# Edge scores of a graph layer: the first half's maximum ahead of the one-hots

## What is computed

```
src = jnp.concatenate([edge_index[0], loops])
dst = jnp.concatenate([edge_index[1], loops])
alpha = jax.nn.leaky_relu(s[src] + s[dst], NEG_SLOPE)
m = jax.ops.segment_max(alpha, dst, num_segments=N)
e = jnp.exp(alpha - m[dst])
denom = jax.ops.segment_sum(e, dst, num_segments=N)
a = e / denom[dst]
msg = Vh[src] * a[:, :, None]
attn = jax.ops.segment_sum(msg, dst, num_segments=N).reshape(N, D_MODEL)
```

## Time and profile before

| what | us |
|---|---|
| median of 3 runs | 2734.74 (2731.53 to 2736.45) |
| the profiled execution | 2739.28 |
| its span, first to last instruction | 2737.2 |
| PE busy | 1815.5 (66%) |
| DVE busy | 1752.0 (64%) |
| POOL busy | 1643.0 (60%) |
| ACT busy | 573.9 (21%) |
| scores of layer one (L690) | 108 to 251 |
| scores of layer two (L690) | 1450 to 1752 |
| messages of layer two (L1164) | 1885 to 2447 |

### The profile page before, as it was taken

One profiled execution on the slowest core, in us unless ns is written; L12 is line 12 of the kernel. 1 busy time (PEld: TensorE's weight loads), 2 busy tenths in 40 slices (PEclk: granted clock), 3 DMA queues, 4 the chain that ended last, 5 costly groups with the idle time before them and its releaser, 6 DMA issues. The chain is left out here.

```text
span 2737.2 us, 36321 instructions
## 1 busy us (share of the span) xinstructions
PE 1815.5 (66%) x10655; PEld 1474.6 (54%) x10655; DVE 1752.0 (64%) x2694; ACT 573.9 (21%) x1106; POOL 1643.0 (60%) x1456
## 2 busy tenths in 40 slices
PE   2795046777655554999886777405677777757688
PEld 1674034555444443699875555403555555546577
DVE  6689335777544447455675666796567777758675
ACT  2463100000000002354412222203000000004454
POOL 3477777887877773100007777788888888850050
PEclk8797567888877776799989999857788889878899
DMA  3266544554333333000023666733454444440010
GB/s 139 58 214 204 178 120 147 167 159 157 105 92 93 92 92 96 1 1 0 18 79 105 213 213 218 244 98 103 152 162 159 158 159 154 132 118 9 5 43 31
DMA packets 118702, 320.73 MB, mean 117 GB/s; under 512 B 37113, under 2 KB 63121, under 8 KB 104811
## 3 DMA queue, kind: packets, MB, share of 16 engines
q0 software_dynamic: 62272, 170.01, 21.9%
q1 hardware_dynamic: 55754, 145.31, 15.1%
q10 hardware_dynamic: 608, 4.59, 0.4%
HBM read 248.70 MB, written 71.12 MB: 117 GB/s over the span
## 5 line engine op out<-in xcount | busy, mean ns | idle before, releaser
L800 POOL DMA_INDIRECT e_ring<-table,e_index x840 | 1081.5, 1288 | 257.6 <-issue 256.1
L1187 PE MATMUL ms_ps_m<-ms_msg,ms_pick 128*128 128x260 f32 (+1 forms) x2816 | 859.7, 474 | 480.3 <-issue 266.5
L1187 PEld LDWEIGHTS ms_ps_m<-ms_msg,ms_pick 128*128 128x128 f32 x2816 | 659.0, 239 | 680.9 <-issue 532.8
L839 POOL DMA_INDIRECT e_ring<-table,e_stage_index x416 | 422.1, 1015 | 125.9 <-issue 120.9
L1164 DVE TENSOR_TENSOR ms_msg<-e_ring,all_xn 128x1040 f32 x176 | 217.8, 1237 | 354.0 <-SPq L1128 354.0
L690 PE MATMUL sc_ps_e<-sc_keys,sc_hot 125*128 125x100 bf16 (+1 forms) x3840 | 280.9, 229 | 86.8 <-DVE all_xn L643 86.5
L690 PEld LDWEIGHTS sc_ps_e<-sc_keys,sc_hot 125*128 125x128 bf16 x3840 | 254.7, 98 | 136.7 <-DVE all_xn L643 109.4
L1164 DVE TENSOR_TENSOR ms_msg<-e_ring,e_weight 128x1056 f32 x176 | 220.6, 1253 | 168.1 <-SPq L1128 168.0
L1160 DVE SCALAR_TENSOR_TENSOR ms_pick<-graph_dst_col,graph_tile_base,graph_lane_row 128x512 f32<-128x512 f32 x352 | 263.1, 748 | 11.4 <-issue 9.8
L605 ACT ACTIVATE sc_rows<-sc_ps_b 125x512 bf16<-125x512 f32 x320 | 173.0, 596 | 322.8 <-PE sc_ps_b L678 321.2
L643 DVE TENSOR_REDUCE all_xn<-sc_ps_e 128x800 f32 (+1 forms) x240 | 229.1, 982 | 1.4 <-PE sc_ps_e L690 1.3
(11 more groups left out here) (421 smaller groups left out, 2668.6 us busy)
## 6 DMA issues: line engine op xcount, KB each, us to landing
ahead<-e_ring SPq DMA_DIRECT2D x32, 1056.0 KB, 4.4
e_ring<-ahead SPq DMA_DIRECT2D x32, 1056.0 KB, 5.0
ahead<-e_ring SPq DMA_DIRECT2D x20, 1040.0 KB, 4.5
e_ring<-ahead SPq DMA_DIRECT2D x20, 1040.0 KB, 5.0
e_ring<-table,e_index POOLq DMA_INDIRECT x840, 2.8
e_ring<-table,e_stage_index POOLq DMA_INDIRECT x416
w_w<-L_ffn_w SPq DMA_DIRECT2D x2, 2048.0 KB
table<-qkv_v SPq DMA_DIRECT2D x5, 528.0 KB
```

Source lines behind the costliest of these rows:

```text
L800: pool.indirect_dma_start(out=g.ring[:, slot * QUAD + i // GT, i % GT, :], out_offset=None, in_=s.table[:, :], in_offset=bass.IndirectOffs ...
L839: pool.indirect_dma_start(out=stage.rows[:, b, t, :], out_offset=None, in_=s.table[:, :], in_offset=bass.IndirectOffsetOnAxis(ap=stage.ind ...
L1187: mm = pe.matmul(ps_m[b][:, 0:W], pick[:, b, t, :], msg[:, b, t, :], start=t == 0, stop=t == GT - 1)
```

## The change

VectorE's order in the scores. `select` now does one half; `turn_item` takes the maxima of all halves but the last, then makes the one-hots of the item after the next, then takes the last half's maximum. The first two items' one-hots are made before the loop, and the last four items stand after it. No wait is dropped or added: each instruction keeps its own condition. The other engines' instructions are the same and in the same order.

```diff
--- before.py
+++ after.py
@@ -636,11 +636,18 @@
                     dve.wait_ge(looked, (it - (HOTS - 1)) * SUBS)
                 dve.tensor_scalar(hot[0:KEYS, q % HOTS, :], rows[0:KEYS, q, :], s.node_of[0:KEYS, 0:1], None, ALU.is_equal).then_inc(hot_ready, 1)
 
-            def select(it, q):
-                for sub in range(SUBS):
-                    dve.wait_ge(looked, it * SUBS + (sub + 1))
-                    found = ps_e[(q * SUBS + sub) % BANKS][:, :].rearrange("p (t c) -> p t c", c=SLOT)[:, :, 0:C].rearrange("p t (g h) -> p t h g", h=H)
-                    dve.tensor_reduce(edge[:, bass.ds(it * ITEM + sub * SL, SL), :], found, AX.X, ALU.max).then_inc(picked, 1)
+            def select(it, q, sub):
+                dve.wait_ge(looked, it * SUBS + (sub + 1))
+                found = ps_e[(q * SUBS + sub) % BANKS][:, :].rearrange("p (t c) -> p t c", c=SLOT)[:, :, 0:C].rearrange("p t (g h) -> p t h g", h=H)
+                dve.tensor_reduce(edge[:, bass.ds(it * ITEM + sub * SL, SL), :], found, AX.X, ALU.max).then_inc(picked, 1)
+
+            def turn_item(it, q, more=True):
+
+                for sub in range(SUBS - 1):
+                    select(it, q, sub)
+                if more:
+                    one_hot(it + HOTS, (q + HOTS) % lanes, False)
+                select(it, q, SUBS - 1)
 
             dve.memset(pair[:, :, :, :], 0.0).then_inc(pair_zero, 1)
             dve.tensor_scalar(which[:, :], s.lane_row[:, :], LOW - 0.5, s.node_of[:, 0:1], ALU.is_ge, ALU.is_equal).then_inc(which_set, 1)
@@ -657,16 +664,13 @@
                 at = first // BANK_HI * TB
                 found = ps_e[0][0:LOW, at:at + (his.stop - his.start) * 3 * H].rearrange("p (g i h) -> p i g h", i=3, h=H)
                 dve.tensor_copy(keys[0:LOW, :, his, :], found).then_inc(keys_ready, 1)
+            for q in range(HOTS):
+                one_hot(q, q, True)
+            with steps_of(dve, 0, NITEM - lanes, lanes) as it0:
+                for q in range(lanes):
+                    turn_item(it0 + q, q)
             for q in range(lanes):
-                one_hot(q, q, True)
-                if q >= 2:
-                    select(q - 2, q - 2)
-            with steps_of(dve, lanes, NITEM, lanes) as it0:
-                for q in range(lanes):
-                    one_hot(it0 + q, q, False)
-                    select(it0 + (q - 2), (q - 2) % lanes)
-            for it in range(NITEM - 2, NITEM):
-                select(it, it % lanes)
+                turn_item(NITEM - lanes + q, q, q + HOTS < lanes)
 
         @block.tensor
         def _(pe):
```

## The result

The changed kernel takes **2740.23 us** (median of 7 runs, 2738.61 to 2746.47), the kernel before 2734.74 (7 runs, 2731.53 to 2736.45): a ratio of 1.0025, 95% interval [1.0014, 1.0037]. Forecast were 2737.9 in a range of 2730 to 2744 and "within 0.2%" as the likeliest outcome. The time lies in the upper part of the range. At a quarter of a per cent slow, the likeliest outcome, "within 0.2%", was narrowly missed on the slow side. The execution that was profiled took 2738.61 us, span 2736.5.

A forecast was written before the change was run, and what follows sets the result against it. The prediction took GpSimd's stream of 628 gathers to bound layer two; −1.6 + 4.8 = +3.2 us on the profiled 2739.28 gave 2742.5, or 2737.9 in terms of the median 2734.74, range 2730 to 2744.

The forecast's parts named there:

- The bound: Layer two ends when GpSimd has issued its 628 gathers, 975.2 us from first to last, which cover the shorter scores.
- Rival A: Message stage of layer two: VectorE's late start sets the end, so 76 us show, 2659 us; with partial gains chance 0.08.
- The period: Scores of layer two: 2.8 us an item against 3.78, so the scores shorten by 76 us and end near 1676.
- The first message product: Start of layer two's message stage: near 1857 us, not 1885, after VectorE stands some 45 us for rows.
- One-hots against gathers, +4.8: Scores of layer two: 80 more closely spaced one-hots lengthen gathers at layer one's price, +4.8 us, bounds 0 and +16.7.
- rival B: Parked gathers in layer two's scores: one-hots always start just ahead of a gather, +15 us, 2750 us; chance 0.15.
- The weights, 0 ± 2: Weights stage and accumulator clearing: VectorE's operations delay gathers as before, their price carried, 0, bounded by ±2 us.
- The first message groups, -1.6: Start of the message stage: without a stock of rows about 10 groups cost gathers 0.62 us each, not 0.78: −1.6 us.
- The sum: End of GpSimd's stream in layer two: −1.6 + 4.8 = +3.2 us, with what follows it unchanged.
- Rivals C and D: C: TensorE's clock falls in layer two's scores, up to 100 us slower, chance 0.02. D: same order, excluded for layer two.
- The page on the ports: GpSimd's gathers: by the skill page only one-hots disturb them, so −1.6 falls away, leaving +4.8 us, 2739.5.
- Wrong if a gather's mean is above 1040 ns: Gathers in layer two's scores: a mean near 1000 ns was expected; above 1040 ns would show one-hots meeting gathers in step.

The follow-up runs named there:

- half_pad_two: The changed kernel with half of the second half's maximum taken twice in each item of layer two: 2738.74 us, ratio 1.0009 to the kernel before.
- half_before: The kernel before with every second gather of both layers left out: 2243.7 us, ratio 0.8198 to the whole kernel before.

## Why the prediction was right, step by step

- **The bound.** Right, and now shown by an experiment: GpSimd's 628 gathers cover the scores. Without half of them 75 us of gain show; with them, none. It holds on the condition in which it was read, though. Rival A (0.08) is what happens on the other chips: 82 us faster.
- **The period.** 2.8 us forecast, 2.76 measured; the scores take 223 us, forecast "about 226", and end at 1669.8, forecast 1676. The two waits shrink to 13% and 22%.
- **The first message product.** 1857 forecast, 1865.7 measured. The step left out the copies of indices (6.2 us in 9), and the dearer one-hots add 3. The sum is not touched by the former.
- **One-hots against gathers, +4.8.** This is the term that was mis-sized: +8.1. The 9.0 us over 80 one-hots are 0.11 us each, not layer one's 0.071. That passes the 0.10 from which rival B was to decide. "2.8 over 1.25 is no whole number" was the argument against B, and it failed: a period of two gathers and 0.26 us still put 43 of 72 one-hots into the dear phase of 0.1 to 0.2 us. B's price of 15 us needed all of them.
- **The weights, 0 ± 2.** -2.0, at the edge. The operation of 9.4 us is again beside a gather of 9.51; the clearing is beside one of 10.83. The cost moved as it was, and one of the copies took part of it over (2 copies, 4.7 us): +1.6 there.
- **The first message groups, -1.6.** -2.6: 14 groups at 0.56 us rather than 0.74. The cause stands (no stock, so no ten groups in a row), but more groups shared in it.
- **The sum.** +3.2 forecast, +3.2 measured in the stream, by terms that were wrong by +3.3 and by -3.3 in all (among them the last 308 gathers, -1.9, taken as unchanged). The hit to a tenth is luck. That the time stays near the old one comes from the bound. That it is a little longer was measured in 7 runs of each, but what makes it longer is read from one trace of each kernel, and half_pad_two, with dearer scores than before and a shorter stream, shows how little that says.
- **Rivals C and D.** The clock held at 0.99 of full speed; the order did change.
- **The page on the ports.** The prediction says that a gather of 9.51 us beside a two-operand instruction does not agree with the Trainium skill, page "SBUF — State Buffer", section "Who interferes with whom". The section has a VectorE instruction with two SBUF inputs contend with a GpSimd instruction that reads SBUF, and the gather reads its row numbers from an SBUF tile (`e_index`, `e_stage_index` in its rows). So the two can agree, and the 2739.5 us worked out "by the page" does not follow from it. The sum did not use it.
- **"Wrong if a gather's mean is above 1040 ns".** It was 1004, near the 1000 forecast. That bound and B's 0.10 us a one-hot did not match: 0.10 × 80 over 155 gathers is 998 ns. The mark to look for should have been worked out with the new number of gathers.

## What to carry to other kernels

Ask first which engine's stream runs across the stage that is made faster, and how much of it is left when the stage ends: here 473 of 628 gathers, so 80 us of a faster stage were worth nothing, and 0.5 us added to each item cost nothing either. The cheapest proof is to halve the covering stream in both kernels. And a change that gains only when the cover fails can still be worth its quarter of a per cent: this one costs 5.5 us in one condition of the chip and brings 74 and 82 us in the other (two pairs).

## What the runs showed of the hardware

- **The same program takes 2735 us on some chips and 3360 on others.** On four of the five chips of the experiments TensorE's products in the scores of both layers raise their semaphore at 2.8 us a product (12 in 33 to 34 us), where 12 take 1.03 us at home, for as long as GpSimd issues gathers, and at the usual pace after. The granted clock meanwhile is 0.50 to 0.53. That the two end together is seen in every trace of those chips. That one causes the other was not tried, and beside the gathers of the message stage TensorE keeps its pace.
- **A large VectorE operation shuts out a gather for its whole length:** a two-operand one of 9.38 us beside 9.51 (9.37 beside 9.51 in the kernel before); a memset of 4.59 us and a product of 5.43, back to back, beside one gather of 10.83. VectorE itself loses nothing by it: without a gather beside them the same three take 9.37, 4.59 and 5.43 us (half_before).

```profile
1719.88 9.38 DVE L1015 TENSOR_TENSOR all_acc<-all_acc,e_dst_line 128x5120 f32<-128x5120 f32 x1 [0.15 <-DVE wt_border L1013]
```

```profile
1720.58 9.51 POOL L843 DMA_INDIRECT e_ring<-table,e_stage_index  x1 [0.30 <-issue]
...
1792.50 10.83 POOL L843 DMA_INDIRECT e_ring<-table,e_stage_index  x1 [0.30 <-issue]
```

- **One-hots and gathers exclude each other for a part of the gather only.** Over the scores of both layers in the five traces from home (683 pairs): one-hots that start 0.13 us ahead of a gather lengthen it by 0.23 us on average, 0.26 us ahead by 0.11, 0.36 us ahead by 0.02, as if it waited for their end. But with the 76 that start 0.1 to 0.3 us behind a gather's start, and so lie wholly beside it, neither side is longer; at 0.4 us the gather is 0.05 longer, at 0.5 and 0.6 the one-hots take 0.65 and 0.60 us instead of 0.49, and from 0.7 on nothing happens. The Trainium skill, page "SBUF — State Buffer", section "Who interferes with whom", has a tensor-scalar in a two-port mode and a GpSimd instruction shut each other out for the whole instruction. Where the one-hots come first the traces fit that; where the gather comes first the 76 pairs do not.
